# Gathered rows handed over in halves of four tiles, in two graph hops and a GIN sum

## What is computed

```python
def _L0_gnn_ref(x, weight, hop_logits, edge_row, edge_col, edge_val):
    support = x @ weight
    hop_w = jax.nn.softmax(hop_logits)
    h1 = spmm(edge_row, edge_col, edge_val, support)
    h2 = spmm(edge_row, edge_col, edge_val, h1)
    return jax.nn.relu(hop_w[0] * h1 + hop_w[1] * h2 + x)
...
def _L1_gnn_ref(x, edge_index, eps, W1, b1, g1, beta1, ...):
    agg = jax.ops.segment_sum(x[src], dst, num_segments=x.shape[0])
    h = (1.0 + eps) * x + agg
    h = jax.nn.elu(_bn(h @ W1 + b1, g1, beta1))
...
    return h @ W4 + b4
...
h = jnp.maximum(_layernorm(x), 0.0)
x = x + _L0_gnn_ref(h, L0_gnn_weight, L0_gnn_hop_logits, src, dst, edge_weight)
h = jnp.maximum(_layernorm(x), 0.0)
x = x + _L1_gnn_ref(h, edge_index, ...)
```

## Time and profile before

| | us |
|---|---|
| time, median of 3 | 4816.79 (4816.38 to 4824.14) |
| time of the profiled execution | 4825.36 |
| its span | 4823.8 |
| PE busy | 3471.2 (72%) |
| DVE busy | 1889.6 (39%) |
| ACT busy | 797.7 (17%) |
| POOL busy | 2726.3 (57%) |
| mean granted clock of TensorE | 0.857 |

### The profile page before, as it was taken

The page is one execution under the profiler, slowest core; times in us unless marked ns, Lnnn a source line. Parts: engine busy times, 40 slices in busy tenths (PEclk is TensorE's granted clock), DMA queues, the critical chain, the costliest instruction groups (busy, mean ns, idle before and its releaser), DMA issues. The chain is left out here.

```text
span 4823.8 us, 48671 instructions
## 1 busy us (share of the span) xinstructions
PE 3471.2 (72%) x15961; PEld 2902.7 (60%) x15961; DVE 1889.6 (39%) x3858; ACT 797.7 (17%) x1968; POOL 2726.3 (57%) x2704
## 2 busy tenths in 40 slices
PE   5758677777777767777777775555555555898998
PEld 4248556566665656666666664555555555687887
DVE  5899532333333323333333332111221211655865
ACT  4048300000000000000000000000000000444766
POOL 0058666766767656766766675777777777101000
PEclk9779888888888878888888887877877787999999
DMA  4000133333333333333333333433333333223323
GB/s 131 0 1 6 47 100 99 101 99 102 101 96 101 98 90 94 106 98 99 101 98 105 99 102 87 146 102 98 99 99 99 98 98 101 83 91 118 106 71 107
DMA packets 187130, 443.80 MB, mean 92 GB/s; under 512 B 49102, under 2 KB 96514, under 8 KB 180714
## 3 DMA queue, kind: packets, MB, share of 16 engines
q0 software_dynamic: 126464, 336.63, 24.0%
q1 hardware_dynamic: 60501, 105.26, 6.3%
HBM read 382.22 MB, written 59.49 MB: 92 GB/s over the span
## 5 line engine op out<-in xcount | busy, mean ns | idle before, releaser
L1848 PE MATMUL ps<-work 128*128 128x256 f32 x6912 | 1783.2, 423 | 635.2 <-DMA work<-table_hop,idx 372.4
L768 POOL DMA_INDIRECT work<-table_hop,idx x1728 | 1654.7, 958 | 766.7 <-issue 718.8
L1848 PEld LDWEIGHTS ps<-work 128*128 128x128 f32 x6912 | 1467.1, 215 | 949.2 <-DMA work<-table_hop,idx 342.6
L811 POOL DMA_INDIRECT work<-table_gin,idx x832 | 834.5, 1003 | 303.0 <-issue 271.0
L1922 PE MATMUL ps<-work 128*128 128x128 f32 x3328 | 571.1, 352 | 488.3 <-issue 260.6
L1922 PEld LDWEIGHTS ps<-work 128*128 128x128 f32 x3328 | 553.6, 264 | 527.4 <-issue 408.9
L1394 DVE TENSOR_SCALAR work<-iota,w_hi,edge_buf 128x256 f32<-128x256 bf16 x1728 | 584.3, 409 | 18.6 <-issue 17.3
L1506 DVE TENSOR_TENSOR sum_b<-sum_b,ps 128x256 f32 x104 | 43.9, 422 | 908.7 <-PE ps L1922 908.7
L1406 DVE TENSOR_TENSOR sum_b<-sum_b,ps 128x512 f32 x108 | 74.2, 687 | 827.5 <-PE ps L1848 827.5
L915 ACT COPY idx<-w 128x8 int32 (+1 forms) x216 | 42.1, 197 | 2135.2 <-PE ps L1848 2093.2
L1406 DVE TENSOR_TENSOR big<-big,ps 128x512 f32 x108 | 74.3, 688 | 797.1 <-PE ps L1848 796.9
(11 more groups left out here) (223 smaller groups left out, 2644.5 us busy)
## 6 DMA issues: line engine op xcount, KB each, us to landing
work<-table_hop,idx POOLq DMA_INDIRECT x1728, 2.7
z_dram<-sum_b SPq DMA_DIRECT2D x24, 1024.0 KB, 3.9
sum_b<-z_dram SPq DMA_DIRECT2D x24, 1024.0 KB, 5.0
work<-table_gin,idx POOLq DMA_INDIRECT x832, 2.7
big<-x SPq DMA_DIRECT2D x12, 512.0 KB, 6.0
table_hop<-work SPq DMA_DIRECT2D x12, 512.0 KB, 2.9
table_hop<-sum_b SPq DMA_DIRECT2D x12, 512.0 KB, 3.4
x_dram<-big SPq DMA_DIRECT2D x12, 512.0 KB, 3.3
```

Source lines behind the costliest of these rows:

```text
L768: pool.indirect_dma_start(hop_rows[:, par, t, :], None, table[n], bass.IndirectOffsetOnAxis(idx[:, k % HR, t:t + 1], 0)).then_inc(hop_in[p ...
L811: pool.indirect_dma_start(rows[:, par, t, :], None, table[2], bass.IndirectOffsetOnAxis(idx[:, q, t:t + 1], 0)).then_inc(gathered[par], 16)
L1848: mm = pe.matmul(ps[:, HWIN * par + b, 0:D], hot[:, par, t, b * P:(b + 1) * P], hop_rows[:, par, t, :], start=(t == 0), stop=(t == GT - 1))
```

## The change

`hop_in[2]` and `gathered[2]` go. Four semaphores `rows_in[par][half]` take their place, used by both hops and by the GIN part. GpSimd waits before each half of four gathers until the same half of group g-2 has been multiplied. TensorE waits before each half of its matmuls for that half's four gathers, and increments `hop_mm` or `mm_done` behind each half, so twice per group. All other waits on these two counters are for twice the number, so they wait for whole groups as before. Tiles, matmuls, DMAs, buffers and the order of everything else stay.

```diff
+HT = GT // 2
...
-        hop_in = [sem("hop_in0"), sem("hop_in1")]
+        rows_in = [[sem(f"rows_in{par}{half}") for half in range(2)] for par in range(2)]
...
-        gathered = [sem("gathered0"), sem("gathered1")]
...
                 pool.wait_ge(hop_idx, g + 1)
-                if not (n == 0 and first and k < 2):
-                    pool.wait_ge(hop_mm, g - 1)
-                pool.sem_inc(pool_opened, 1)
-                for t in range(GT):
-                    pool.indirect_dma_start(hop_rows[:, par, t, :], None, table[n],
-                                            bass.IndirectOffsetOnAxis(idx[:, k % HR, t:t + 1], 0)).then_inc(hop_in[par], 16)
+                for half in range(2):
+                    if not (n == 0 and first and k < 2):
+                        pool.wait_ge(hop_mm, 2 * (g - 2) + half + 1)
+                    pool.sem_inc(pool_opened, 1)
+                    for t in range(half * HT, (half + 1) * HT):
+                        pool.indirect_dma_start(hop_rows[:, par, t, :], None, table[n],
+                                                bass.IndirectOffsetOnAxis(idx[:, k % HR, t:t + 1], 0)
+                                                ).then_inc(rows_in[par][half], 16)
...
-                    act.wait_ge(hop_mm, g - HR + 1)
+                    act.wait_ge(hop_mm, 2 * (g - HR + 1))
...
-                    dve.wait_ge(hop_mm, g - 1)
+                    dve.wait_ge(hop_mm, 2 * (g - 1))
...
                 pe.wait_ge(hop_hot, g + 1)
-                pe.wait_ge(hop_in[par], 16 * GT * (n * HGROUPS // 2 + HBODY // 2 * i + k // 2 + 1))
                 if not (n == 0 and first and k < 2):
                     pe.wait_ge(hop_add, g - 1)
-                for t in range(GT):
-                    for b in range(HWIN):
-                        mm = pe.matmul(ps[:, HWIN * par + b, 0:D], hot[:, par, t, b * P:(b + 1) * P],
-                                       hop_rows[:, par, t, :], start=(t == 0), stop=(t == GT - 1))
-                mm.then_inc(hop_mm, 1)
+                for half in range(2):
+                    pe.wait_ge(rows_in[par][half], 16 * HT * (n * HGROUPS // 2 + HBODY // 2 * i + k // 2 + 1))
+                    for t in range(half * HT, (half + 1) * HT):
+                        for b in range(HWIN):
+                            mm = pe.matmul(ps[:, HWIN * par + b, 0:D], hot[:, par, t, b * P:(b + 1) * P],
+                                           hop_rows[:, par, t, :], start=(t == 0), stop=(t == GT - 1))
+                    mm.then_inc(hop_mm, 1)
```

More of the change, by code:

```diff
@@ L619, in x1_out @@
                 if paced:
-                    sp.wait_ge(mm_done, 2 * i + q + 1)
+                    sp.wait_ge(mm_done, 2 * (2 * i + q + 1))
                     sp.sem_inc(sp_opened, 1)
@@ L806, in gin_gather @@
                 pool.wait_ge(idx_ready, RING * i + q + 1)
-                if not (first and q < 2):
-                    pool.wait_ge(mm_done, RING * i + q - 1)
-                pool.sem_inc(pool_opened, 1)
-                for t in range(GT):
-                    pool.indirect_dma_start(rows[:, par, t, :], None, table[2],
-                                            bass.IndirectOffsetOnAxis(idx[:, q, t:t + 1], 0)).then_inc(gathered[par], 16)
+                for half in range(2):
+                    if not (first and q < 2):
+                        pool.wait_ge(mm_done, 2 * (RING * i + q - 2) + half + 1)
+                    pool.sem_inc(pool_opened, 1)
+                    for t in range(half * HT, (half + 1) * HT):
+                        pool.indirect_dma_start(rows[:, par, t, :], None, table[2],
+                                                bass.IndirectOffsetOnAxis(idx[:, q, t:t + 1], 0)
+                                                ).then_inc(rows_in[par][half], 16)
             def low_of_w1(j, u):
@@ L959, in fill @@
                 if not first:
-                    act.wait_ge(mm_done, g - RING + 1)
+                    act.wait_ge(mm_done, 2 * (g - RING + 1))
                 act.wait_ge(edges_ready, 1)
@@ L1401, in add_hop @@
                 at_ = dve.value_load(win_i[0:1, bass.ds(HBODY * i + k, 1)], min_val=0, max_val=(NT - HWIN) * D)
-                dve.wait_ge(hop_mm, g + 1)
+                dve.wait_ge(hop_mm, 2 * (g + 1))
                 if not (n == 0 and first and k == 0):
@@ L1491, in build @@
                 if not (first and q < 2):
-                    dve.wait_ge(mm_done, g - 1)
+                    dve.wait_ge(mm_done, 2 * (g - 1))
                 loc = dst_loc[:, bass.ds(g * GT, GT)].unsqueeze(2).to_broadcast([P, GT, WIN])
@@ L1501, in add @@
                 base = dve.value_load(base_i[0:1, bass.ds(g, 1)], min_val=0, max_val=ROWS - WIN)
-                dve.wait_ge(mm_done, g + 1)
+                dve.wait_ge(mm_done, 2 * (g + 1))
                 if not (first and q == 0):
@@ L1916, in group @@
                 pe.wait_ge(onehot_ready, g + 1)
-                pe.wait_ge(gathered[par], 16 * GT * (2 * i + q // 2 + 1))
                 if not (first and q < 2):
                     pe.wait_ge(evac_done, g - 1)
[L1920 to L1924, removed]
+                for half in range(2):
+                    pe.wait_ge(rows_in[par][half], 16 * HT * (HGROUPS + 2 * i + q // 2 + 1))
+                    for t in range(half * HT, (half + 1) * HT):
+                        for a in range(DH):
+                            mm = pe.matmul(ps[:, 2 * par + a, 0:WIN], rows[:, par, t, a * P:(a + 1) * P],
+                                           onehot[:, par, t, :], start=(t == 0), stop=(t == GT - 1))
+                    mm.then_inc(mm_done, 1)
             with pe.If(near):
```

## The result

The changed kernel takes 4579.9 us (median of 4 runs, 4574.6 to 4583.0), the kernel before 4816.6 (4815.2 to 4824.1). The ratio is 0.950, 95% interval 0.9487 to 0.9514. On the profiled executions the difference is 4825.4 - 4579.4 = 246.0 us.

A forecast was written before the change was run, and what follows sets the result against it. GpSimd's gather issues and their waits for buffers were taken to bound the hops. Gains of 175.3 + 0 + 1.8 + 9.0 + 1.0 = 187.1 us turned the median 4816.8 into 4629.7 us, range 4608 to 4672.

The forecast's parts named there:

- What bounds the hops: Both hops: GpSimd's gather issues plus its wait at every second group for buffers held until group g-2 is multiplied.
- The loop through one buffer: Hops: issue, landing, matmuls and restart take 22.56 us against 20.05 for sixteen issues; halves make it 10.9 to 14.1.
- The 175.3 us: Hops: excess of 53 late gathers per hop, 90.5 and 84.8 us, expected to go whole with halves.
- No other wait took their place: Rival in the hops: part of the wait returns under another name, a third left, 58 us, 4688; chance 0.07.
- The stalls after 112 issues: Hops, inside groups: sixteen GpSimd stalls of 2.2 to 2.3 us, 31 over the ordinary gap, expected to stay.
- The part on the change: Instructions added: 320 waits and increments on GpSimd, one more of each per group on TensorE; taken as 0 us.
- The handshakes: Rival on GpSimd: each added wait and increment costs 0.30 us, 96 in all, giving 4726; chance 0.03.
- GIN: GIN part: start gains 1.8 us, bounds 0 to 3.6; nothing to gain for the other 102 groups.
- some 14 us that can shift: GpSimd's mean issue of 0.958 against the common 0.95 us leaves this amount, which new overlap can shift.
- The ends: Last groups' matmuls shorten: 4.5 us for each hop, 9.0 together, and 1.0 in GIN, bounds 0 to 1.9.
- The clock: Hops' matmuls expected at full clock; rival that TensorE stays at 1.2 GHz: 551 us more, 5368, chance 0.04.
- The range: Whole kernel: 4608 to 4672 us, taking in the forecast and the milder half of the returning-wait rival; forecast chance 0.84.

The follow-up runs named there:

- x3_take_halves: Kernel before with four row semaphores, TensorE taking rows in halves, GpSimd getting them back by whole groups: 4586.5 us beside 4820.8, ratio 0.9519.
- x4_give_halves: Changed kernel, but TensorE starts only when all eight tiles are there; rows still given back in halves: 4613.8 us beside 4820.8, ratio 0.9572.
- x2_four_sems: Kernel before with four row semaphores in place of two, rows taken and given back by whole groups: 4807.5 us beside 4820.8, ratio 0.9973.
- y3_hops_only: Changed kernel with GIN's two semaphores and whole groups restored, so only the hops are changed: 4616.8 us beside 4823.7, ratio 0.9569.
- y1_short_mm: Kernel before with 9 of a hop group's 16 matmuls, sums not the reference's, two semaphores kept: 4657.8 us in one run, beside 4823.7.
- z1_short_four: Kernel before with 9 of a hop group's 16 matmuls, whole groups, and four row semaphores: 4610.1 us in one run, beside 4815.7.
- x1_mid_wait: Kernel before with only a met wait and an increment added on GpSimd before each group's fifth gather: 4821.6 us beside 4820.8, ratio 0.9998.
- the quarters: Changed kernel handing over two tiles at a time with eight row semaphores: 4594.8 us beside 4823.7; again 4587.5, beside the changed kernel's 4579.6.

## Why the prediction was too cautious, point by point

**What bounds the hops: right.** The loop through one buffer made every second group late, and its working holds in both directions (x3_take_halves, x4_give_halves): taking in halves alone and giving back in halves alone each bring it under 20.05 us, and each leaves no late gather. The 175.3 us went whole. No other wait took their place.

**The stalls after 112 issues: the step that failed.** The prediction counted them, called them there "whatever the data do", took 31 us of them in the hops out of the sum as fixed, left GIN's seven out altogether, and said that only they would be left. (It counted sixteen; fifteen are of 2.2 to 2.3 us, the sixteenth is the 1.59 us at the start.) They are not fixed. They were worth 29.2 us in the hops and 13.5 in GIN, 42.7 of the 58.9 us by which the profiled difference exceeds the sum, and that is why a hop spans 1089 us in place of the 1105 expected. They depend on how many semaphores the gathers count on, which the change raises from two to four. In GIN this alone is enough: seven stalls become one of 1.19 us with four semaphores (x2_four_sems), and with its two semaphores restored all seven are back (y3_hops_only). In the hops it takes both parts of the change. Their stalls, over the ordinary gaps and without the first, are:

| hops | late gathers | no late gathers |
|---|---|---|
| two semaphores | 29.2 us (before) | 30.2 (y1_short_mm) |
| four semaphores | 14.2 (x2_four_sems) | 3.7 (z1_short_four), 0 (the changed kernel) |

The trace of before held a hint. The hops share two semaphores, and the count of 112 runs on from one hop into the other. GIN has two of its own, and the count starts anew: from the last stall of hop 2, with 46 gathers still to come behind it, to the first of GIN, ahead of its 114th gather, it is 160 gathers.

```profile
2901.29 0.94 POOL L768 DMA_INDIRECT work<-table_hop,idx  x1 [2.25 <-issue]
...
3148.99 0.94 POOL L811 DMA_INDIRECT work<-table_gin,idx  x1 [2.33 <-issue]
```

The part on the change named the four semaphores and asked only what the added waits cost. A term for the semaphores that the gathers increment was missing, and its bounds should have reached to a gain: the rows gave no reason why a stall with a strict period in the number of DMAs should be independent of the bookkeeping of DMAs.

**The handshakes: right.** 320 more waits and increments on GpSimd cost nothing that can be measured: the upper end of the interval of x1_mid_wait, 1.0007, is 3.4 us, against a bound of 96. In its trace and in that of the changed kernel the mean gap ahead of a group's fifth gather is 0.30 us like the others.

**GIN: the size was off.** The start gained 1.6 us (1.8 predicted). "For the other 102 groups nothing can be gained" was wrong twice: by the stalls, and by 11.8 us of shorter issues. In the trace of before 89 of GIN's issues take over 1.05 us, 46.0 us over 0.95 in all, and each of the 89 overlaps VectorE's one-hot build (L1495), as do 87 that are not longer; in the changed kernel it is 67 and 34.6 us, which is nearly the whole difference. That TensorE's releases now let VectorE build at other moments is the likely reason for the smaller number; it was not tested by itself. The prediction had this only as "some 14 us that can shift"; its sign could not be told from the trace of before, and the quarters show that it goes the other way as easily. Together with the hops' 4.2 it came to 16.0.

**The ends: right in size for the hops, wrong for GIN.** Between the stages 10.7 us are saved (9.0 predicted). At GIN's end nothing was (1.0 predicted, bounds 0 to 1.9): the last half's 16 records run at a granted clock of 0.50 and take as long as the 32 of the earlier trace rows did at 1.00.

```profile
3859.06 3.78 PE L1928 MATMUL ps<-work 128*128 128x128 f32 x16 [3.06 <-DMA work<-table_gin,idx]
```

**The clock: right for the hops.** Their granted clock rose to 0.99 and 0.97, with pauses of 1.3 us twice in a group; with quarters, four pauses of about 0.5 us a group, it was 0.99 to 1.00. So the rule of the Trainium skill, page "TensorE: Matmul & The Clock Gate", section "A second HAM failure mode: psum-queue depth-cycling", that frequent short pauses make the clock swing, is not borne out by the hops here. GIN stayed at 0.78, after 0.79.

**The range: too narrow below.** Its lower end held every gain that the sum had a term for, and 14 us. The stalls were no term of it; with their 42.7 us the sum would have given 4587, beside the 4579.9 measured.

## What to carry to other kernels

Follow one buffer once around its loop (issue, landing, work, restart) and compare the sum with the time at which the slot is wanted again: this named the waits of 175 us, and all of them went. Handing over in halves pays until the loop is shorter than the stream of issues, and either side of the hand-over can be enough, as here; the quarters gained nothing more and moved the work of other engines against each other. A gap that comes with a strict period in the number of DMAs can hang on what the DMAs count on, as it does here, so a change to their semaphores has to be priced against it, not only against the waits. Whether its count starts anew where the semaphores change can be read from the trace before anything is built.

## What the runs showed of the hardware

- In these kernels gathers issued by GpSimd on two semaphores stop once every 112 issues for about 1.95 us over the ordinary gap of 0.30, in the hops and in GIN, and with late gathers or without. The next gather starts 3.2 us after the start of the one before it; the page's median from an issue to its landing is 2.7. With four semaphores the stops that remain are 104 issues or a multiple of it apart, the longest of them (2.04 to 2.07 us) right behind late gathers; with eight they are gone but for two gaps of 0.38 us. What GpSimd waits for there is in no row, and why more semaphores help stays open.
- A satisfied semaphore wait with an increment between two gathers adds nothing to their 1.25 us.
- Whether an issue on GpSimd is delayed by VectorE's 128x1024 float32 operation (1.28 us, two inputs in SBUF) depends on its start. In hop 1 of the kernel before, the changed kernel and both runs of quarters, every issue that starts 0.13 to 0.97 us behind the start of the operation ends 0.8 us after its end, so it takes 1.13 to 1.98 us; every other issue that overlaps it takes 0.94 or 0.95.
